# A mixture-of-experts kernel: expert lists in units of 128 rows, with split tiles in front

## The reference

```
logits = einsum('th,eh->te', x, router_w)            # 8192 tokens, 8 experts
topk_logits, topk_idx = top_k(logits, 2)
probs = softmax(topk_logits)
combine[t, topk_idx] += probs
hmid = gelu(einsum('th,efh->etf', x, w1) + b1)       # 256 -> 512
y = einsum('etf,ehf->eth', hmid, w2) + b2            # 512 -> 256
out = einsum('eth,te->th', y, combine)
```

## Time and profile before

| | |
|---|---|
| median of 3 runs | 1095.82 us (1094.07 to 1098.82) |
| profiled execution, span from the first to the last instruction | 1089.8 us |
| median less span | 6.0 us |
| PE busy | 951.3 us, 87% |
| DVE busy | 831.0 us, 76% |
| POOL busy | 699.4 us, 64% |
| ACT busy | 660.6 us, 61% |
| PE's clock over the span | 0.963 of 2.4 GHz |
| indirect adds to the output | 142, mean 1589 ns on POOL |
| loads of a tile's rows | 71 of 260 KB, 3.0 us to landing |

### The profile page before, as it was taken

How to read it: one execution, slowest core, us unless ns; L and a number is a source line. 1 busy time by engine, 2 the same in 40 slices (tenths; PEclk the granted TensorE clock), 3 DMA queues, 4 the chain that set the end, 5 groups by cost and what they waited for, 6 DMA issues and landing times. The chain is left out here.

```text
span 1089.8 us, 33554 instructions
## 1 busy us (share of the span) xinstructions
PE 951.3 (87%) x10092; PEld 784.3 (72%) x10093; DVE 831.0 (76%) x2201; ACT 660.6 (61%) x1253; POOL 699.4 (64%) x606
## 2 busy tenths in 40 slices
PE   4599888988898898888889833999999999999995
PEld 2377667766766775675677733999999999999994
DVE  5378999998997997997999874666666666666663
ACT  5667776776776677666767432555555555555552
POOL 5626677786677678776778553556556565566555
PEclk9799999999998999998999966999999999999998
DMA  3665886446654654673655282455555555555554
GB/s 111 149 142 125 274 178 156 126 153 161 165 126 137 159 132 135 155 173 98 164 139 139 89 316 97 89 90 96 96 96 88 87 98 96 97 85 95 92 97 49
DMA packets 129125, 140.30 MB, mean 129 GB/s; under 512 B 12512, under 2 KB 122208, under 8 KB 128416
## 3 DMA queue, kind: packets, MB, share of 16 engines
q1 hardware_dynamic: 101184, 102.38, 38.0%
q0 software_dynamic: 26688, 35.93, 17.8%
q10 hardware_dynamic: 1184, 1.18, 0.3%
HBM read 72.01 MB, written 67.44 MB: 128 GB/s over the span
## 5 line engine op out<-in xcount | busy, mean ns | idle before, releaser
L1497 POOL DMA_INDIRECT out<-yt,to_token x142 | 225.7, 1589 | 172.8 <-DVE yt L1360 108.6
L792 ACT ACTIVATE ahl<-pS 128x512 f16<-128x512 f32 x240 | 141.0, 599 | 74.7 <-PE pS L508 73.1
L1035 DVE SCALAR_TENSOR_TENSOR ahl<-pS,ahl 128x512 f16<-128x512 f32 x240 | 161.2, 682 | 28.8 <-ACT ahl L792 27.5
L1414 POOL DMA_INDIRECT expert_in<-xn,cur x128 | 130.5, 1020 | 35.1 <-issue 33.1
L960 ACT ACTIVATE g<-pS,b1s 128x256 f32<-128x256 f32 x144 | 60.2, 470 | 90.7 <-PE pS L433 90.7
L433 PE MATMUL pF<-xT,was 128*128 128x512 f16 x384 | 102.7, 410 | 11.8 <-DVE xT L1040 11.8
L505 PE MATMUL pS<-cbs 128*128 128x512 bf16 x240 | 93.0, 387 | 20.2 <-DVE ahl L1035 12.2
L1331 DVE TENSOR_TENSOR ghl<-g,ghl 128x1024 f16<-128x1024 f32 x71 | 87.1, 1227 | 24.3 <-ACT ghl L982 24.3
L433 PE MATMUL pU<-w2s,ghl 128*128 x864 | 100.5, 273 | 1.9 <-DVE ghl L1331 1.9
L433 PE MATMUL pS<-gT,w1s 128*128 128x256 f16 x864 | 101.1, 274 | 0.1
L433 PE MATMUL pF<-w2s,ghl 128*128 x840 | 97.4, 273 | 0.0
(11 more groups left out here) (160 smaller groups left out, 2323.9 us busy)
## 6 DMA issues: line engine op xcount, KB each, us to landing
xg<-expert_in SPq DMA_DIRECT2D x71, 260.0 KB, 3.0
qk_parts<-qkhl SPq DMA_DIRECT2D x32, 512.0 KB, 2.9
qst<-qk_parts SPq DMA_DIRECT2D x96, 128.0 KB
kst<-qk_parts SPq DMA_DIRECT2D x48, 256.0 KB
xs<-x SPq DMA_DIRECT2D x16, 512.0 KB, 4.6
xr<-x SPq DMA_DIRECT2D x16, 512.0 KB, 4.8
out<-x SPq DMA_DIRECT2D x16, 512.0 KB, 3.2
expert_in<-pads SPq DMA_DIRECT2D x16, 260.0 KB, 3.7
```

Of the source, the lines that this page charges most:

```text
L792: nc.scalar.activation(ahl[:, b % 2, 0, n * 4 * C:(n + 1) * 4 * C], score_bank(fr, n)[:], ACT.Relu).then_inc(sc_hi, 1)
L1035: V.scalar_tensor_tensor(ahl[:, b % 2, 1, cols], score_bank(fr, n)[:], 0.0, ahl[:, b % 2, 0, cols], ALU.max, ALU.subtract).then_inc(sc_lo, 1)
L1414: G.indirect_dma_start(xg_dram, bass.IndirectOffsetOnAxis(ap=cur[:, qp, 2 * b + t:2 * b + t + 1], axis=0), xn2[:, qp, b], None).then_inc(s ...
L1497: G.indirect_dma_start(out, bass.IndirectOffsetOnAxis(ap=to_token[:, c % 2, s:s + 1], axis=0), yt[:, c % 2, s], None, compute_op=ALU.add). ...
```

## The change

Lists are cut in units of 128 rows. 16384 rows in eight lists need at most 135 units (`UNITS`). 64 tiles (`FULL`) take two units of one expert each, as before; the up to 7 units that remain (`SINGLES`, at most one per list, but for a case with eight of them that `ninth` treats) are put in four tiles (`SPLIT`) in front of them: tile 0 holds one unit and tiles 1 to 3 two each, of different experts. `NT` becomes 68; `NS` = 71 is the number of table entries (slots). For a split tile SP makes a DMA for each unit, the hidden layer runs for each half of 128 columns with its expert's weights, Gelu and the bias once for each half. Between the halves of a split tile, and between split tiles, POOL waits for the landing of the add before. The table chain has 30 steps. PE's second layer waits for `y_biased` of two tiles before where it waited for `y_done`. Copies and subtractions of whole tiles are written as slices.

```diff
-NT = (2 * T + E * (MT - 1)) // MT
+UNITS = (2 * T + E * (P - 1)) // P
+FULL = 2 * T // MT
+SINGLES = UNITS - 2 * FULL
+SPLIT = (SINGLES + 1) // 2
+NT = SPLIT + FULL
+NS = SINGLES + FULL
+DUMMY_UNITS = 4 * MT
...
-        TAB = 18
+        TAB = 30
...
         def tiles(engine, body, first=-2):
-            for c in range(first, 2):
+            for c in range(first, SPLIT):
                 body(0, c)
-            with engine.Fori(0, (NT - 5) // 2) as j:
-                for c in (2, 3):
+            with engine.Fori(0, (FULL - 2) // 2) as j:
+                for c in (SPLIT, SPLIT + 1):
                     body(j, c)
-            for c in range(2 + (NT - 5) // 2 * 2, NT):
+            for c in range(NT - 2, NT):
...
+        def is_split(j, c):
+            return isinstance(j, int) and c < SPLIT
+        def halves(j, c):
+            return 1 if is_split(j, c) and c == 0 else 2
+        def slots(j, c):
+            if is_split(j, c):
+                return [2 * c - 1 + h if c else 0 for h in range(halves(j, c))]
+            return [2 * j + c + NS - NT]
...
+        def added_of(j, c):
+            return ADDED0 + 32 * (j + c // 2 + 1) - 16 * (c % 2 == 0)
...
+                for h, row in enumerate(rows):
+                    part = xg[:, c % 2, h:h + 1] if is_split(j, c) else xg[:, c % 2]
+                    sp.dma_start(part, xg_dram[bass.ds(row, size), :].rearrange("(s p) d -> p s d", p=P)).then_inc(xg_in[c % 2], 16)
...
+                    experts = [pe.value_load(table[0:1, 1, bass.ds(n, 1)], min_val=0, max_val=E - 1) for n in slots(j, c + 1)]
+                    width = P if is_split(j, c + 1) else MT
...
+                        for h, e in enumerate(experts):
+                            c0 = h * P
+                            mm = split3(hidden[p1][f // 2][:, (f % 2) * MT + c0:(f % 2) * MT + c0 + width],
+                                        lambda a, k: w1s[:, a, bass.ds(e * KC + k, 1), f * P:(f + 1) * P].rearrange("p e f -> p (e f)"),
+                                        lambda a, k: gT[:, p1, a, k * MT + c0:k * MT + c0 + width], KC)
...
-                        pe.wait_ge(y_done, t - 1)
-                    for s in range(MT // P):
+                        pe.wait_ge(y_biased, biased_of(j, c - 2))
...
-                        nc.scalar.activation(g[:, p1, f], hidden[p1][f // 2][:, (f % 2) * MT:(f % 2 + 1) * MT], ACT.Gelu,
-                                             bias=b1s[:, bass.ds(e * FC + f, 1)], scale=1.0 / WS).then_inc(gelu, 1)
+                        for h, e in enumerate(experts):
+                            c0 = (f % 2) * MT + h * P
+                            nc.scalar.activation(g[:, p1, f, h * P:h * P + width], hidden[p1][f // 2][:, c0:c0 + width], ACT.Gelu,
+                                                 bias=b1s[:, bass.ds(e * FC + f, 1)], scale=1.0 / WS).then_inc(gelu, 1)
...
-                    nc.scalar.activation(gT[:, c % 2, 0], rows_T[c % 2][:], ACT.Copy).then_inc(gt_hi, 1)
+                    n = halves(j, c + 2) * P
+                    nc.scalar.activation(gT[:, c % 2, 0].rearrange("p (k n) -> p k n", k=KC)[:, :, 0:n],
+                                         rows_T[c % 2][:].rearrange("p (k n) -> p k n", k=KC)[:, :, 0:n], ACT.Copy).then_inc(gt_hi, 1)
...
+            units, pairs, lone, pair_row, lone_row, upto_lone = [tiles_f[:, n] for n in (1, 3, 4, 5, 6, 7)]
+            tri = cfs[:, C_TRI8:C_TRI8 + E * E].rearrange("p (a b) -> p a b", a=E)
+            chain(V.tensor_tensor(upto, tiles_f[:, 2].unsqueeze(1).to_broadcast([P, E, E]), tri, ALU.mult))
+            chain(V.tensor_reduce(upto_pair[:, 1:1 + E], upto, AX.X, ALU.add))
+            chain(V.tensor_scalar(upto_pair[:, 1:1 + E], upto_pair[:, 1:1 + E], float(FULL), None, ALU.min))
+            chain(V.tensor_tensor(pairs, upto_pair[:, 1:1 + E], upto_pair[:, 0:E], ALU.subtract))
+            chain(V.scalar_tensor_tensor(lone, pairs, -2.0, units, ALU.mult, ALU.add))
...
+            V.tensor_tensor(past[:, 0:SINGLES], number[:, 0:SINGLES].unsqueeze(2).to_broadcast([P, SINGLES, E]),
+                            upto_lone.unsqueeze(1).to_broadcast([P, SINGLES, E]), ALU.is_ge)
+            chain(V.tensor_tensor(past[:, SINGLES:NS], number.unsqueeze(2).to_broadcast([P, FULL, E]),
+                                  upto_pair[:, 1:1 + E].unsqueeze(1).to_broadcast([P, FULL, E]), ALU.is_ge))
             chain(V.tensor_reduce(tj[:, 0], past, AX.X, ALU.add))
-            chain(V.tensor_tensor(past_tiles, past, mine.unsqueeze(1).to_broadcast([P, NT, E]), ALU.mult))
-            chain(V.tensor_reduce(tj[:, 1], past_tiles, AX.X, ALU.add))
-            chain(V.tensor_tensor(tj[:, 2], number, tj[:, 1], ALU.subtract))
-            V.tensor_scalar(tile_expert[:], tj[:, 0], float(E - 1), None, ALU.min)
-            chain(V.tensor_scalar(tj[:, 3], tj[:, 0], float(CAP), None, ALU.mult))
-            chain(V.scalar_tensor_tensor(table[:, 0], tj[0:1, 2], float(MT), tj[0:1, 3], ALU.mult, ALU.add))
+            V.tensor_tensor(past_rows[:, 0:SINGLES], past[:, 0:SINGLES], lone_row.unsqueeze(1).to_broadcast([P, SINGLES, E]), ALU.mult)
+            V.tensor_tensor(past_rows[:, SINGLES:NS], past[:, SINGLES:NS], pair_row.unsqueeze(1).to_broadcast([P, FULL, E]), ALU.mult)
+            chain(V.tensor_tensor(past_pairs, past[:, SINGLES:NS], pairs.unsqueeze(1).to_broadcast([P, FULL, E]), ALU.mult))
+            chain(V.tensor_reduce(tj[:, 1], past_rows, AX.X, ALU.add))
+            chain(V.tensor_reduce(tj[:, 2, 0:FULL], past_pairs, AX.X, ALU.add))
...
+            V.tensor_scalar(settled[:, 0], first_i[:, 0], 32.0, float(added_of(0, SPLIT - 2)), ALU.mult, ALU.add)
+            chain(V.tensor_scalar(settled[:, 1], first_i[:, 1], 32.0, float(added_of(0, SPLIT - 1)), ALU.mult, ALU.add))
...
-                    V.tensor_tensor(gT[:, c % 2, 1], rows_T[c % 2][:], gT[:, c % 2, 0], ALU.subtract).then_inc(gt_lo, 1)
+                    n = halves(j, c + 2) * P
+                    low_high = [x.rearrange("p (k n) -> p k n", k=KC)[:, :, 0:n] for x in (gT[:, c % 2, 1], rows_T[c % 2][:], gT[:, c % 2, 0])]
+                    V.tensor_tensor(*low_high, ALU.subtract).then_inc(gt_lo, 1)
                 if is_tile(j, c + 1):
                     p1 = (c + 1) % 2
+                    n = halves(j, c + 1) * P
                     dve.wait_ge(g_hi, t + 2)
-                    V.tensor_tensor(ghl[:, p1, 1].rearrange("p f n -> p (f n)"), g[:, p1].rearrange("p f n -> p (f n)"),
-                                    ghl[:, p1, 0].rearrange("p f n -> p (f n)"), ALU.subtract).then_inc(g_lo, 1)
+                    V.tensor_tensor(ghl[:, p1, 1, :, 0:n], g[:, p1, :, 0:n], ghl[:, p1, 0, :, 0:n], ALU.subtract).then_inc(g_lo, 1)
...
-                        dve.wait_ge(added[c % 2], ADDED0 + 32 * (j + c // 2))
-                    V.scalar_tensor_tensor(yt[:, c % 2], y_bank[c % 2][:].rearrange("p (s d) -> p s d", s=2), 1.0 / WS,
-                                           b2s[:, bass.ds(e, 1)].to_broadcast([P, 2, D]), ALU.mult, ALU.add).then_inc(y_biased, 1)
-                    dve.wait_ge(y_biased, t + 1)
-                    for s in range(MT // P):
+                        dve.wait_ge(added[c % 2], added_of(j, c - 2))
+                    for h, e in enumerate(experts):
+                        rows, n = (slice(h, h + 1), 1) if is_split(j, c) else (slice(0, 2), 2)
+                        V.scalar_tensor_tensor(yt[:, c % 2, rows], y_bank[c % 2][:].rearrange("p (s d) -> p s d", s=2)[:, rows], 1.0 / WS,
+                                               b2s[:, bass.ds(e, 1)].to_broadcast([P, n, D]), ALU.mult, ALU.add).then_inc(y_biased, 1)
...
-                even = pool.value_load(settled[0:1, 0, bass.ds(t, 1)], min_val=ADDED0, max_val=ADDED0 + 16 * (NT + 1))
-                odd = pool.value_load(settled[0:1, 1, bass.ds(t, 1)], min_val=ADDED0, max_val=ADDED0 + 16 * (NT + 1))
+                if not is_split(j, c):
+                    even, odd = [pool.value_load(settled[0:1, n, bass.ds(t - SPLIT, 1)], min_val=added_of(0, SPLIT - 2 + n),
+                                                 max_val=ADDED0 + 16 * (NT + 1)) for n in range(2)]
...
-                pool.wait_ge(added[0], even)
-                pool.wait_ge(added[1], odd)
+                n = halves(j, c)
+                G.tensor_copy(to_token[:, c % 2, 0:n], row_token[:, bass.ds(t, 1), 0:n].rearrange("p t s -> p (t s)")).then_inc(token_copy, 1)
+                if not is_split(j, c):
+                    pool.wait_ge(added[0], even)
+                    pool.wait_ge(added[1], odd)
+                elif c >= 1:
+                    pool.wait_ge(added[(c - 1) % 2], added_of(j, c - 1))
                 pool.wait_ge(token_copy, t + 1)
-                pool.wait_ge(y_done, 2 * t + 2)
+                pool.wait_ge(y_done, done_of(j, c))
                 carry_wait(pool)
-                for s in range(MT // P):
+                for s in range(n):
+                    if is_split(j, c) and s:
```

(18 more changed lines are left out.)

116 lines of the change are left out of this document (70 added, 46 removed).

## The result

The changed kernel takes 1088.84 us (median of 6 runs, 1085.21 to 1093.1) where the kernel before, on the same chip, takes 1096.64 (6 runs): 7.8 us less between the medians; the ratio is 0.9927 [0.9905, 0.9948]. Forecast were 11.0 us less.

The account below looks back on a forecast made before the run. The prediction took PE's dense matmuls, 5.68 us a tile, to bound the expert half. Its terms, -17.0 - 2.1 - 1.75 + 8.8 + 1.0 = -11.0 us, gave 1084.8 us; own range 1081 to 1088, wide range 1076 to 1092.

Parts of the forecast that it names:

- Fewer tiles, -17.0: Expert half: 71 tiles become 68, saving three periods of 5.68 us on PE's path, padding or not: -17.0 us.
- rival 5: Padding tiles might be cheaper than a period, so dropping them saves less; chance 0.03 together with the unforeseen.
- The chain, 11.3 us long, and -2.1 at the first layer: DVE's longer table chain delays w2, so fewer POOL scatters are slowed and the first hidden layer starts earlier: -2.1 us.
- Tile 0 is one half, -1.75: From tile 0's to tile 2's hidden layer, PE saves half of both layers of tile 0: -1.75 us.
- Split tiles, 128 columns at 55 ns, cost 0: Hidden layers of tiles 1 to 3: 48 matmuls of 128 columns take 2.6 us, weight loads hidden: cost 0.
- The bound of 6.5 us: Upper bound for the split tiles' cost, if each 128-column matmul took 109 ns again.
- Matmuls over 60 ns apart: Profile sign: 128-column matmuls spaced this widely would mean that weight loads are not hidden under them.
- rival 2: Split tiles: weight loads run in series with 128-column matmuls, 82 ns a pair, +3.3 us, 1088.1 us; chance 0.18.
- The adds, h = 5.0 and +8.8: POOL's split-tile adds form a serial chain, 5.0 us per link (h), delaying tile 6's bias and PE: +8.8 us.
- The clock, +1.0: Gaps in PE during the adds' stalls, about 3, 4 and 1 us, may drop its clock: +1.0 us.
- The rest, 0: PE's second-layer wait, split loads as two DMAs and the unchanged end on a padding tile: cost 0.
- rival 4: The 64 pair tiles slow down through copies and subtractions over sliced views; 1110 us at 1.0 us each; chance 0.06.

Follow-up runs that it names:

- experiment 5: The kernel before with 68 tiles instead of 71 and nothing else, enough for these inputs: 1080.16 us, ratio 0.9857.
- experiment 6: The kernel before with 21 more chained small DVE steps at the end of the table chain, so w2's low half starts later: 1094.72 us, ratio 0.9978.
- experiment 1: The changed kernel with PE's weights in split tiles fixed to experts 0 and 1, at constant addresses (output wrong there): 1087.24 us, ratio 0.9904.
- experiments 2: The changed kernel with split tiles' adds sent to separate padding rows, without POOL's waits between them (real rows lack them): 1087.87 us, ratio 0.9909.
- experiment 8: The changed kernel with four result buffers (yt) instead of two, order of adds kept: 1086.82 us, ratio 0.991.
- after: The changed kernel itself, as profiled in one execution: median time 1088.84 us, ratio 0.9927 to the kernel before.
- experiment 7: The changed kernel with w2's low half moved later, two pieces behind tile 0's rows and two behind tile 1's: 1088.64 us, ratio 0.9919.
- experiment 9: The changed kernel with four result buffers and the split units' experts read into registers once, early, on PE and ACT: 1078.62 us, ratio 0.9821.
- experiment 4: The changed kernel with the split units' experts read into registers once, before tile 0, on PE, ACT and DVE: 1089.56 us, ratio 0.9924.

## Why the prediction was right, and where its steps were not

The time came 4.0 us above the forecast 1084.8, just above the forecast's own range of 1081 to 1088 and inside the wide one. One large term came out right for a reason that held only in part, so the nearness is in part luck. Step by step:

*Fewer tiles, -17.0.* Right: experiment 5 gives 17.0 by the back half. That padding tiles cost as much as others, rival 5's point, is shown with it.

*The chain, 11.3 us long, and -2.1 at the first layer.* 11.2 us, and -1.2 (+23.94 against +25.17). The mechanism is right, and experiment 6 shows it alone (-2.3 at the first layer, for a step of 8.90 us that begins 5.3 later). Mis-sized: the last scatter ends at +16.5, where I had 662.5 - 646.57 = +15.9; the load begins 1.9 us behind its end (669.24 - 667.38), which I had as 1.7; and from there to the first layer it is 0.2 longer than before.

*Tile 0 is one half, -1.75.* Wrong: from tile 0 to tile 2 it is 11.08 us, before 10.60, so +0.5. In experiment 1 it is 9.1, a gain of 1.5: the idea was right, and the split tile 1 ate it, with 48 slow matmuls (1.6 us) and a pause of 0.64.

*Split tiles, 128 columns at 55 ns, cost 0.* **This is the step that failed.** I took from the earlier trace rows that weights load within 28 ns, and that is so: with fixed addresses the pair takes 56 ns. What I left out was the queue. The register steps are in the trace of the kernel before as well; I had counted PE's matmuls and not what stands between them. Per split tile they cost 1.6 us of spacing, and up to 0.9 us for each layer's two reads. The bound of 6.5 us, for all of it, was too low: without the chain 8.1 us stand over the pace from tile 2 to tile 9 (experiments 2 and 8), and some 2 come in tile 1; it allowed for slow weights in the array and for no reads. Matmuls over 60 ns apart were to speak for rival 2, and they are 87 apart; but with fixed addresses they are 56 apart, so weights do load beside 128 columns, and rival 2 is refuted as a mechanism. The Trainium skill, "TensorE: Matmul & The Clock Gate", section Back-to-back issue gap, gives about 81 ns for such a pair; the runs here show 56 with fixed addresses and 87 with computed ones, so its figure is neither, and the 1088.1 us of rival 2 lies near the result by another cause than the one it named.

*The adds, h = 5.0 and +8.8.* The links measured 4.63 in after and (74.07 - 44.25) / 6 = 4.97 in experiment 1, where the start isn't held back; the first link in after, 4.01 us with POOL's restart in it, has no load beside it (the queues move 33 GB/s in it, 55 to 90 in the others), so I had a clean link too long (4.45) and the mean about right. As a mechanism the term is right: experiment 1, in which PE is fast, shows gaps of about 3, 1 and 2.5 us, where I had 3, 4 and 1, and 10.9 us lost. As a term of a sum it was wrong, since PE in after is late itself, and the chain adds 2.5.

*The clock, +1.0.* In after it did not fall in this stage: the one gap of 1.91 us is followed by a layer at full pace (1.51). In experiment 1 it fell twice, behind the gaps of 2.87 and 2.49 us, as forecast for the stalls described; the slow layers are 1.6 and 1.7 us longer than 2.78, more than the 1.0 that I had. In experiment 7 it fell behind a gap of 1.98 us.

*The rest, 0.* Right: 58 periods at 5.68 refute rival 4; the end is 21.2 us behind the last hidden layer, before 21.5.

The sum by what was measured: -17.0 - 1.2 + 0.5 + 10.3 - 0.2 = -7.6. Against my -11.0 the 3.4 us are 0.9 of the chain of w2, 2.2 of tile 0, 0.5 of the stretch behind, and -0.2. That the stretch fits to 0.5 us is no proof of its step: **two causes of equal size lay over each other, and I had one of them.**

The sizes inside the stretch: of the 7.8 us that tiles 2 to 4 lose to PE, slow spacing gives 2 x 1.58 = 3.2 and pauses 3.0 (1.5 + 1.3 + 1.1 in the view of waits, less 0.64 and 0.24 ahead of tile 2). The other 1.6 stand as idle time on no row, but they belong to the reads: from tile 2's hidden layer to tile 5's experiment 8 takes 24.8 us and experiment 9, with early reads, 20.3, which is 3.3 over three periods and no more than the spacing. Two things stay open. What makes one link of the chain 4 us long and another 6 or more is not separated by any run. And why the clock stayed up behind the gap of 1.91 us in after and fell behind that of 1.98 in experiment 7 the runs don't show.

## What to carry to other kernels

Before halving the width of instructions on a dense engine, count its queue as well as its array: register steps, reads and matmuls, each by its own duration in the trace, against the time of the array; what was hidden at one width may bound at half of it. Where a stall is forecast, work out also what else in the same stretch grew, since side by side two limits cost the larger one, and removing either alone gains little (2.0 and 2.5 us here, 12.8 together). A serial chain of DMAs need not be shortened: two more result buffers and reads done ahead gained 9.8 us with the chain in place.

## What the runs showed of the hardware

- A pair of a 128x128 weight load and a matmul of 128 columns in f16 comes every 56 ns at full clock with constant addresses (24 in 1.50 us), every 87 ns with two register steps of 46 ns per three pairs (48 in 4.32 us).
- Reading a number from a table into a register takes PE 0.30 + 0.15 us in its queue, and DVE's seven reads in a row 5.0 us.
- From the issue of an indirect add to the issue of the next one, which waits for its landing, it takes 3.76 us at the shortest (experiment 4) and 6.94 at the longest (experiment 9); 4.63 on average in after.
- An indirect scatter takes POOL 0.96 us, 1.2 to 1.5 beside DVE steps of 0.7 us and 1.9 to 3.0 beside steps of 2.3 us that read two tiles of SBUF; such a scatter ends 0.82 to 0.84 us behind the end of the step that it met. The Trainium skill, "SBUF — State Buffer", section SBUF: two separate sides, states that a DVE instruction with two SBUF inputs and a GpSimd instruction that reads SBUF exclude each other: whichever starts first has a shared pair of ports until it ends. The ends of the scatters agree with that, and the load starts 2.9 us earlier where w2 moves off (experiment 7); the ports themselves stand in no trace.
- Behind a gap of PE of 1.91 us the granted clock stayed at 1.00 (after); behind gaps of 1.98, 2.49 and 2.87 us it was 0.53 to 0.61 over the 12 or 24 matmuls that followed (experiments 7 and 1).
